# Attention loop of a transformer layer: one filler matmul per step taken out, the bias copy moved from VectorE to ScalarE

## The reference

```python
xn = _layernorm(x, axis=-1)
# attention: 32 half-heads of 32 dims, 16 heads, values of 64 dims
q = (xn @ Wq.T).reshape(b, t, 32, 32).transpose(0, 2, 1, 3) * 32 ** -0.5
k = (xn @ Wk.T).reshape(b, t, 32, 32).transpose(0, 2, 1, 3)
v = (xn @ Wv.T).reshape(b, t, 16, 64).transpose(0, 2, 1, 3)
aw = softmax(einsum('bhqd,bhkd->bhqk', q, k)).reshape(b, 16, 2, t, t)
aw = aw[:, :, 0] - lam * aw[:, :, 1]
attn = einsum('bhqk,bhkd->bhqd', aw, v)
attn = attn * rsqrt(mean(attn * attn) + EPS) * g * (1 - LAMBDA_INIT)
attn = attn.transpose(0, 2, 1, 3).reshape(b, t, 1024) @ Wo.T
# feed-forward, 1024 -> 4096 -> 4096 -> 4096 -> 1024
h = silu(lin(xn, w1)) * lin(xn, w2)
h = gelu(lin(h, h1)); h = gelu(lin(h, h2))
return x + attn + lin(h, w3)
```

## Time and profile before

| | |
|---|---|
| median of 2 runs | 6556.8 us (6556.3 to 6557.3) |
| profiled execution, its own time | 6559.2 us |
| span of its slowest core (core 7) | 6557.6 us |
| spans of the 8 cores | 6548.8 to 6557.6 us |
| mean granted TensorE clock of the cores | 0.948 to 0.949 |
| PE busy | 5933.7 us, 90% |
| ACT busy | 2794.7 us, 43% |
| DVE busy | 1533.7 us, 23% |

### The profile page before, as it was taken

One profiled execution on the slowest core, in us unless ns is written; L12 is line 12 of the kernel. 1 busy time (PEld: TensorE's weight loads), 2 busy tenths in 40 slices (PEclk: granted clock), 3 DMA queues, 4 the chain that ended last, 5 costly groups with the idle time before them and its releaser, 6 DMA issues.

```text
span 6557.6 us, 71624 instructions; the slowest of 8 cores (6548.8 to 6557.6 us)
## 1 busy us (share of the span) xinstructions
PE 5933.7 (90%) x26144; PEld 2274.1 (35%) x26144; DVE 1533.7 (23%) x2078; ACT 2794.7 (43%) x2872; POOL 170.8 (3%) x325
## 2 busy tenths in 40 slices
PE   2599899899898998998998989999999899999997
PEld 1233233233232332332332334444444344444443
DVE  7423333332333223333233332000000110000001
ACT  3377477576574784774875751100000011000000
POOL 0000000000000000000000001000000010000000
PEclk9899899899898998998998999999999899999998
DMA  2100000000000000000000005544444354444343
GB/s 84 33 1 1 7 1 4 3 1 7 1 1 7 1 1 7 1 1 14 1 1 1 1 29 90 85 77 77 73 76 82 82 100 84 77 77 77 75 85 88
DMA packets 76596, 247.95 MB, mean 38 GB/s; under 512 B 8608, under 2 KB 25056, under 8 KB 57824
## 3 DMA queue, kind: packets, MB, share of 16 engines
q0 software_dynamic: 44000, 193.03, 16.6%
q1 hardware_dynamic: 32256, 50.35, 2.4%
HBM read 419.50 MB, written 16.78 MB: 67 GB/s over the span
## 4 chain that ended last, share of the span: by engine, by line
PE 76%; DVE 15%; ACT 4%; issue 3%; DMA 1%; DVEq 0%; ACTq 0%; SPq 0%; POOLq 0%
PE pM L910 27%; PE psS L516 13%; PE psO L532 5%; PE psO L536 5%; PE psA L391 4%; PE psA L558 4%; PE psB L558 4%; PE pM L982 4%; PE pM L843 3%; PE pM L856 3%; DVE rows L615 3%; DVE rows L606 3%; ACT e L572 2%; DVE smll L479 2%; ACT rows L653 1%
## 5 line engine op out<-in xcount | busy, mean ns | idle before, releaser
L910 PE MATMUL pM<-a,hbT 128*128 128x512 bf16 x8192 | 1770.4, 379 | 8.9 <-DVE a L875 6.1
L516 PE MATMUL psS<-xn_own,identb 128*128 128x512 bf16 x4096 | 1620.9, 396 | 0.0
L572 ACT ACTIVATE e<-psA,bias_gp 128x1024 bf16<-128x1024 f32 x1024 | 1143.0, 1116 | 710.3 <-PE psA L558 686.0
L572 ACT ACTIVATE e<-psB,bias_gp 128x1024 bf16<-128x1024 f32 x1024 | 1143.0, 1116 | 266.7 <-PE psB L558 241.9
L910 PEld LDWEIGHTS pM<-a,hbT 128*128 128x128 bf16 x8192 | 801.7, 98 | 977.6 <-issue 13.0
L532 PE MATMUL psO<-e,vgt 128*65 128x512 bf16 x2048 | 801.5, 391 | 46.2 <-DVE o1s L596 46.2
L536 PE MATMUL psO<-e,vgt 128*65 128x512 bf16 x2048 | 797.3, 389 | 0.0
L516 PEld LDWEIGHTS psS<-xn_own,identb 128*128 128x128 bf16 x4096 | 402.0, 98 | 735.6 <-issue 552.7
L1007 DVE TENSOR_TENSOR f3s<-f3s,asld 128x1024 f32<-128x1024 f32 x16 | 19.6, 1226 | 2040.3 <-ACT f3s L1001 2040.3
L558 PE MATMUL psA<-qg,kg 32*128 32x512 bf16 x2048 | 406.7, 393 | 43.1 <-ACT e L572 43.0
L923 ACT ACTIVATE a<-pM,h2ss 128x1024 bf16<-128x1024 f32 x64 | 71.4, 1116 | 815.8 <-PE pM L910 815.8
(11 more groups left out here) (122 smaller groups left out, 3219.4 us busy)
## 6 DMA issues: line engine op xcount, KB each, us to landing
hbT<-h POOLq DMA_DIRECT2D x128, 1024.0 KB, 8.9
w12b<-w POOLq DMA_DIRECT2D x128, 256.0 KB, 4.8
ph0x<-x SPq DMA_DIRECT2D x32, 512.0 KB, 3.6
hbT<-w POOLq DMA_DIRECT2D x16, 1024.0 KB, 8.9
xldp<-x SPq DMA_DIRECT2D x128, 64.0 KB, 2.0
asld<-attn_scr SPq DMA_DIRECT2D x16, 512.0 KB, 3.9
out<-outT SPq DMA_DIRECT2D x16, 512.0 KB, 3.1
attn_scr<-wosb SPq DMA_DIRECT2D x16, 256.0 KB, 3.1
```

What stands on the lines that cost most here:

```text
L516: prog.do("tensor", lambda e: e.matmul(pwarm, identb, xn_own[:, 0:512], start=True, stop=True), waits=[(sv, marks.get("stat_v", 0)), (sa, ...
L572: e.activation(e01[kp3], Sps, AF.Exp, bias=bias_gp[:, p:p + 1]),
L910: ic=ic, hc=hc, srcap=srcap: e.matmul(pp[:, 512 * hc:512 * (hc + 1)], w[:, 128 * ic:128 * (ic + 1)], srcap[:, TCH * ic + 512 * hc: TCH * i ...
```

## The change

In the attention loop the second `emit_warm()` of a step, the one ahead of `emit_av`, is gone; the one ahead of the scores stays. Of the 4096 filler matmuls 2048 are left. The 16 copies of the bias (L506) go from VectorE to ScalarE, as an activation with the function Copy, and those that wait for them wait for ScalarE's semaphore.

```diff
                         waits=[(sv, m_mh_v), (sv, m_evac_prev), (sg, m_init),
-                               (sv, bias_a.get(0, 0))],
+                               (sa, bias_a.get(0, 0))],
                         incs=[(st, 1)])
                     mt = st.n
-                    prog.do("vector", lambda e, p=p_: e.tensor_copy(
-                        bias_gp[:, p:p + 1], pb),
+                    prog.do("scalar", lambda e, p=p_: e.activation(
+                        bias_gp[:, p:p + 1], pb, AF.Copy),
                         waits=[(st, mt)] + marks.pop("biastap", []))
-                    bias_a[p_] = sv.n
+                    bias_a[p_] = sa.n
...
-                                          (sv, m_bias_a), (sv, m_vgt_v)]
+                                          (sa, m_bias_a), (sv, m_vgt_v)]
...
                         tqv, tk = divmod(t_, 32)
-                        emit_warm()
                         emit_av(tk, t_ % 3)
```

More of the change, by code:

```diff
@@ L502, in build @@
                         waits=[(sv, m_mh_v), (sv, m_evac_prev), (sg, m_init),
-                               (sv, bias_a.get(0, 0))],
+                               (sa, bias_a.get(0, 0))],
                         incs=[(st, 1)])
                     mt = st.n
-                    prog.do("vector", lambda e, p=p_: e.tensor_copy(
-                        bias_gp[:, p:p + 1], pb),
+                    prog.do("scalar", lambda e, p=p_: e.activation(
+                        bias_gp[:, p:p + 1], pb, AF.Copy),
                         waits=[(st, mt)] + marks.pop("biastap", []))
-                    bias_a[p_] = sv.n
+                    bias_a[p_] = sa.n
                 if "bias" in taps and g == 0:
                     mkb = sdma.issue(lambda e: e.dma_start(
-                        taps["bias"], bias_gp), waits=[(sv, bias_a[1])])
+                        taps["bias"], bias_gp), waits=[(sa, bias_a[1])])
                     marks["biastap"] = [mkb]
```

## The result

The changed kernel took 6,595.6 us (median of 18 runs), before 6,558.7 us (17 runs); the ratio is 1.0055, with a 95% interval of 1.0033 to 1.0077. By the bound of 2% that is no change; it is half a per cent slower. A ratio leaves out runs in which the cores of a die ran slower than the others, a median doesn't, so the two needn't agree to the last digit. The profiled execution took 6,568.5 us and its slowest core, core 6, had a span of 6,566.9 us. It lay at the lower edge of the runs; its cores ranged from 6,548.5 to 6,566.9 us.

A forecast was written before the change was run, and what follows sets the result against it. PE was taken to set the pace at 1.29 us per step. A block of 43.28 + 3.8 = 47.1 us against 47.06 gave 6556.8 + 3 + 0.7, said as 6560 us, range 6,430 to 6,770.

The forecast's parts named there:

- ACT becomes the pace, at 1.21 us: Attention step: without the filler PE needs 1.06 us, below ACT's 1.21, so a step gains 0.08 us.
- A block at full clock is 43.28 us: Attention block, summed part by part: 43.28 us against 46.11 before, 2.83 us less, 181 us over 64 blocks.
- The wait at `mk_c2` grows from 1.73 to about 2.9 us, and each is followed by a fall: PE reaches `mk_c2` earlier while DVE doesn't: wait about 2.9 us, one fall of the clock in every block.
- `mk_c5` brings a new wait of about 1.7 us and falls in two of three blocks: `mk_c5`'s two ACT instructions stop PE for 1.54 us plus 0.15; the clock falls in two of three blocks.
- 1.67 falls per block of 6.0 us, 0.38 us lost per us at the low clock: 3.8 us: Clock price in the attention loop: 1.67 falls x 6.0 us x 0.38 gives 3.8 us per block.
- The sum: 47.1 us per block, 6,560 us: Attention block 43.28 + 3.8 = 47.1 us against 47.06; whole kernel 6,560 us, the gain given back by the clock.
- The bias copy: 0.7 us: 16 copies ahead of the first scores, each 0.05 us longer on ACT: 0.7 us; table loads at most 21 us.
- The rival with a clock that swings all through the loop: Attention loop: 0.15 us idle per step lowers the clock repeatedly; block 53.1 us, kernel about 6,940 us; chance 0.06.
- The rival that the clock stays low for longer: Behind `mk_c2` and `mk_c5` the thinner loop raises the clock late: 10 us stretches, 6,722 us; chance 0.22, extreme included.
- the break-even of 9.9: Low-clock time per attention block at which the gain is used up: 43.28 + 0.38 T = 47.06, T = 9.9 us.
- Its extreme: The clock never comes up in the attention loop: block 61.4 us, kernel over 7,470 us; chance 0.04.

## Why the prediction was right, step by step

- *ACT becomes the pace, at 1.21 us.* Right, 1.21 in the rows. PE's own step was said to be 1.06 us and is 1.09; at the low clock 1.96, as said.
- *A block at full clock is 43.28 us.* The changed kernel has no such block. The run with both waits filled shows it by itself: 43.35 us. The parts of the changed kernel's blocks without low clock agree with it: 13.26 us from `mk_c2` to `mk_c5` and 19.55 from there to the copy, against 13.27 and 19.54 in that run. So the gain before the clock's cost, 2.83 us per block, was sized within 0.1 us.
- *The wait at `mk_c2` grows from 1.73 to about 2.9 us, and each is followed by a fall.* 2.74 us in the row, 144.2 / 56 = 2.58 on average, and 55 falls in 56 waits. The share that I read for before, 0.61 or about two thirds, was 40 of 56, 0.72.
- *`mk_c5` brings a new wait of about 1.7 us and falls in two of three blocks.* The wait is 1.41 us where I show it and 1.5 on average, and the falls are 27 for 56: about half. Filling one wait and not the other showed that it is a cause by itself.
- *1.67 falls per block of 6.0 us, 0.38 us lost per us at the low clock: 3.8 us.* There were 1.49 falls of 8.0 us, 11.9 us low, and they cost 47.49 - 43.35 = 4.14 us, 0.35 per us. The count and the loss per us were somewhat too high and the length too short, and they offset each other in part: that the cost came out so near is luck to that extent. For the length I had named the thinner step; the sorted falls say that the larger part is that half of them come while PE still waits.
- *The sum: 47.1 us per block, 6,560 us.* 47.49 and, at the profiled execution, 6,568.5. The median of the runs is another 27 us higher. Two things weren't in the sum. First, it priced all 64 blocks alike. The 56 blocks lost 0.44 us each, 25 us in all, but the eight first blocks of the groups, from their first exponential to the copy, went from 47.06 to 44.47 us and gained 21, so the loops grew by only 4 us in the profile. I hadn't foreseen either; that they offset each other is luck. Second, the time is the slowest of eight cores: in this profile the cores' spans lie 18 us apart, against 9 before, and up to 95 us in other runs, since each core has its own series of falls. Over the runs that the ratio uses the slowest core lies 23 us above the mean of the eight, against 5 for the kernel before (twelve runs taken beside the repeat of the changed kernel). These 18 us are about half of the 36 by which I was low.
- *The bias copy: 0.7 us.* Its chain became 0.02 us shorter, not 0.05 longer; the table loads that I kept as an upper bound aren't there: the run with the copy alone has the same five loads as before, none of them in a group. That it costs some 30 us through the falls is likely, and why is the open point above.
- *The rival with a clock that swings all through the loop*, which the Trainium skill's rule would have made of it (TensorE: Matmul & The Clock Gate, section "A second HAM failure mode: psum-queue depth-cycling"), fell with the filled waits: a step takes 1.21 us there and PE's part of it 1.09, so PE has its short idle time in each step as in the changed kernel, and the clock is 1.00. That rule speaks of short idle times that come with every iteration; these runs don't agree with it for this loop, where the falls came behind single waits of 1.4 us and more.
- *The rival that the clock stays low for longer* was nearest: 11.9 us per block is beyond the break-even of 9.9 that I gave and short of the 15.3 for 2%. Its extreme exists, one filler further on: 0.50 but for a few short rises, 6,877 us.

## What to carry to other kernels

A matmul whose result nobody reads can be what holds the clock, so don't cost it only at its own length: look at the granted clock behind PE's waits, and ask of any edit that makes PE faster which waits it lengthens. Here an estimated 181 us of gain were given back by the low clock behind waits of 1.4 to 2.7 us, and came back as soon as these were filled or their cause was moved. Filler did most in the waits, where it cost next to nothing (0.15 us per block), and best is a wait that isn't there: one semaphore mark set one instruction earlier made the kernel before 2.5% faster, and together with the halved filler 5.4% (interval 4.4 to 6.4%).

## What was not expected of the hardware

The clock stayed at 0.50 or 0.51 through the attention loops while PE was busy 354 of 364 us in a stretch, with two score matmuls of 32 rows and two value matmuls in each 1.53 us step and no full 128x128 one. PE's busy share didn't tell whether the clock would rise; with one 128x128 filler in the step it rose, after 8.0 us on average. Whether it is the filler's size or just one matmul more isn't shown, since no run has a smaller one in its place. I hadn't expected either that the spread between cores that compute the same would grow from 9 us to 18 and more through the clock alone.
